# Sliding-window attention: convolutions that read the projections in PSUM, with the bias carried in closed form

## The reference

```
q = x @ Wq.T + bq ; k = x @ Wk.T + bk ; v = x @ Wv.T + bv      # x is layer-normalised first
y[t] = sum_i w[:, i] * q[t - 3 + i] + b                        # causal depthwise convolution, 4 taps,
                                                               # rows before t = 0 are zeros; also for k and v
q, k = rotary(q, k) ; q = l2norm(q) ; k = l2norm(k)
scores = q k^T / 8 , allowed where j <= i and i - j < 64
out = softmax(scores) @ v
x = x + out @ Wo.T + bo
```

## Time and profile before

| | |
|---|---|
| median of 3 runs | 2964.65 us (2958.33 to 2971.37) |
| the profiled execution | 2957.25 us, span 2955.9 us |
| the sliding attention within it, first projection to last update of x | 855 to 1337 us |
| first pairs of the two streams (A and B start 33 us apart) | 855 and 888 to 1093 and 1099 us |
| second pairs (start 5 us apart) | 1098 and 1103 to 1335 and 1337 us |

### The profile page before, as it was taken

One profiled execution on the slowest core, in us unless ns is written; L12 is line 12 of the kernel. 1 busy time (PEld: TensorE's weight loads), 2 busy tenths in 40 slices (PEclk: granted clock), 3 DMA queues, 4 the chain that ended last, 5 costly groups with the idle time before them and its releaser, 6 DMA issues. The chain is left out here.

```text
span 2955.9 us, 40949 instructions
## 1 busy us (share of the span) xinstructions
PE 2287.9 (77%) x15598; PEld 1476.6 (50%) x15598; DVE 1866.6 (63%) x3594; ACT 1356.9 (46%) x2546; POOL 695.9 (24%) x610
## 2 busy tenths in 40 slices
PE   4777839574948887885888689766778989779889
PEld 1222439454934544453586368445455554555554
DVE  6989824493438978879898899753562242652331
ACT  4545304231427877873652464344334333435342
POOL 2727340404042212216591066000010100100000
PEclk9989969786969998996897699778789999899899
DMA  4000047304832111110000000202000000000000
GB/s 175 0 0 1 1 134 234 99 1 152 241 93 87 43 33 40 40 33 5 0 1 1 0 1 1 70 1 68 13 1 1 1 2 1 8 1 1 1 1 7
DMA packets 70708, 117.80 MB, mean 40 GB/s; under 512 B 9616, under 2 KB 46224, under 8 KB 70160
## 3 DMA queue, kind: packets, MB, share of 16 engines
q1 hardware_dynamic: 64112, 104.69, 12.0%
q0 software_dynamic: 4096, 8.40, 0.9%
q10 hardware_dynamic: 2304, 2.10, 0.3%
HBM read 84.61 MB, written 16.78 MB: 34 GB/s over the span
## 5 line engine op out<-in xcount | busy, mean ns | idle before, releaser
L185 DVE SCALAR_TENSOR_TENSOR conv<-conv_in,held_l1a,conv 128x512 f32<-128x512 f32 x288 | 244.2, 871 | 29.4 <-ACT conv L166 26.4
L179 POOL TENSOR_TENSOR long<-long,product 128x512 f32<-128x512 f32 x136 | 214.1, 1593 | 198.9 <-ACT product L166 190.4
L209 POOL MEMSET wide_q<- 128x1536 f32 x8 | 11.0, 1379 | 887.1 <-DVE stream_b L182 837.3
L179 POOL TENSOR_TENSOR part<-state,c_rows 128x512 f32<-128x512 f32 x128 | 161.1, 1285 | 72.1 <-issue 53.0
L179 POOL TENSOR_TENSOR qk<-conv,held_const 128x512 f32<-128x512 f32 x64 | 92.3, 1443 | 349.4 <-DVE conv L185 349.4
L182 DVE TENSOR_SCALAR grown<-grown 128x512 f32<-128x512 f32 x92 | 39.6, 430 | 210.6 <-ACT grown L166 163.7
L148 PE MATMUL ps<-part,held_const 128*128 128x512 f32 x256 | 147.1, 659 | 13.3 <-POOL part L179 8.4
L191 DVE TENSOR_TENSOR_SCAN state<-decay,ps 128x512 f32<-128x512 f32 x128 | 146.9, 1193 | 0.0
L188 DVE TENSOR_REDUCE wide_q<-ps 128x4 f32<-128x512 f32 (+1 forms) x128 | 113.5, 950 | 49.8 <-PE ps L148 49.8
L166 ACT ACTIVATE probs<-ps 128x768 f32<-128x768 f32 x128 | 96.5, 808 | 88.2 <-PE ps L148 88.0
L148 PE MATMUL ps<-yn,nT 128*128 128x192 f32 (+2 forms) x640 | 115.6, 313 | 20.3 <-DVE yn L179 17.6
(11 more groups left out here) (503 smaller groups left out, 6135.2 us busy)
## 6 DMA issues: line engine op xcount, KB each, us to landing
ring_a<-in_experts SPq DMA_DIRECT2D x46, 512.0 KB
ring_b<-in_experts SPq DMA_DIRECT2D x46, 512.0 KB
turned<-conv SPq DMA_DIRECT2D x256, 64.0 KB
ring<-lags SPq DMA_DIRECT2D x64, 128.0 KB
held_l3f<-in_l3f SPq DMA_DIRECT2D x1, 2824.0 KB
xg<-rows_x_a SPq DMA_DIRECT2D x10, 256.0 KB
xg<-rows_x_b SPq DMA_DIRECT2D x10, 256.0 KB, 5.2
rows_y_a<-y SPq DMA_DIRECT2D x10, 256.0 KB, 5.4
```

The costliest lines, as they stand in the source:

```text
L179: return self.vector(self.real.tensor_tensor(out, a, b, op), columns(out), out, a, b)
L185: return self.vector(self.real.scalar_tensor_tensor(out, a, p, b, first, second), columns(out) + 60, out, a, b)
L209: return self.vector(self.real.memset(out, value), columns(out) // 2, out)
```

## The change

`conv_in` and the copy are gone. ScalarE's one activation reads the projection in PSUM and writes tap 3 (the unshifted one) with one bias, `whole`: the projection bias times the sum of the four taps, plus the convolution bias. VectorE adds taps 0, 1 and 2 directly from PSUM, each to the columns from 3, 2 and 1 on. Since `whole` counts the bias in all four taps, a fourth, small operation adds `gone` (minus the bias times the missing taps) to the first three columns of both sequences. `whole` and `gone` are made once per pair by seven small VectorE operations. `s.convolved` now counts four for each tile. Bank 1 comes free after the fourth (`free[0] = s.convolved, TAPS * (k + 1)`). The order of the programs changes too: on TensorE the projection of k stands behind the first mix, that of v behind the second score, and both lengths behind the second mix. ScalarE's begins and roots are moved to match. The diff, without renamed counts:

```diff
-    b = a.many(conv_in=[P, 2, SEQS, 3 + T], conv=[P, 4, TOK], turned=[P, 2, TOK], qk=[P, 2, 2, TOK],
+    b = a.many(sums=[P, 2, 3 * CT], gone=[P, 3, 3 * CT], whole=[P, 3 * CT], conv=[P, 4, TOK], turned=[P, 2, TOK], qk=[P, 2, 2, TOK],
...
+    TAPS = 4
+    tap = lambda i: w.l1_taps.rearrange("p (j i) -> p i j", i=TAPS)[:, i, :]
...
-            free[0] = s.copied, k + 1
+            free[0] = s.convolved, TAPS * (k + 1)
...
             yield from score(2 * g)
             if more:
                 yield from project(3 * g + 3)
-                yield from project(3 * g + 4)
             yield from mix(2 * g)
             if more:
+                yield from project(3 * g + 4)
+            yield from score(2 * g + 1)
+            if more:
                 yield from project(3 * g + 5)
-            yield from score(2 * g + 1)
+            yield from mix(2 * g + 1)
             if more:
                 yield from lengths_q(g + 1)
                 yield from lengths_k(g + 1)
-            yield from mix(2 * g + 1)
-            if more:
                 yield from turn_v(g + 1)
             yield from give(g)
...
-        def copy(k):
+        def begin(k):
             g, r = divmod(k, 3)
             j = r * CT + g
+            yield act.wait_ge(s.prepared, 5)
             yield act.wait_ge(s.projected, k + 1)
-            yield act.wait_ge(s.cleared, 1)
-            if k >= 2:
-                yield act.wait_ge(s.convolved, 3 * (k - 1))
-            act.activation(b.conv_in[:, k % 2, :, 3:], seqs(st.ps(1)), ACT.Identity,
-                           bias=w.l1_bqkv[:, j:j + 1]).then_inc(s.copied)
-            yield act.wait_ge(s.copied, k + 1)
             if k >= 4:
                 before = k - 4
                 if before % 3 == 2:
@@ -1302,12 +1299,12 @@
                 else:
                     yield act.wait_ge(s.cosed, 2 * (before // 3) + before % 3 + 1)
                     yield act.wait_ge(turns[before % 3], 64 * (turned_before + before // 3 + 1))
-            act.activation(seqs(b.conv[:, place(k), :]), b.conv_in[:, k % 2, :, 0:T], ACT.Identity,
-                           bias=w.l1_tap_bias[:, j:j + 1], scale=w.l1_taps[:, 4 * j:4 * j + 1]).then_inc(s.begun)
+            act.activation(b.conv[:, place(k), :], st.ps(1), ACT.Identity, bias=b.whole[:, j:j + 1],
+                           scale=w.l1_taps[:, TAPS * j + 3:TAPS * j + 4]).then_inc(s.begun)
...
             yield from exps(2 * g)
             if more:
-                yield from copy(3 * g + 3)
-                yield from copy(3 * g + 4)
+                yield from begin(3 * g + 3)
             yield from invert(2 * g)
             if more:
+                yield from begin(3 * g + 4)
                 yield from square(g + 1, 0)
             yield from exps(2 * g + 1)
             if more:
-                yield from copy(3 * g + 5)
+                yield from begin(3 * g + 5)
                 yield from square(g + 1, 1)
-                yield from roots(g + 1)
             yield from invert(2 * g + 1)
             if more:
+                yield from roots(g + 1)
                 yield from keep_v(g + 1)
...
-        ve.memset(b.conv_in[:, :, :, 0:3], 0.0).then_inc(s.cleared)
+        step = Steps(s.prepared)
+        yield step(ve.tensor_tensor(b.sums[:, 1, :], tap(0), tap(1), ALU.add))
+        yield step(ve.tensor_tensor(b.sums[:, 0, :], b.sums[:, 1, :], tap(2), ALU.add))
+        yield step(ve.tensor_tensor(b.whole[:, :], b.sums[:, 0, :], tap(3), ALU.add))
+        yield step(ve.tensor_tensor(b.whole[:, :], b.whole[:, :], w.l1_bqkv, ALU.mult))
+        ve.scalar_tensor_tensor(b.gone[:, 0:2, :], b.sums[:, 0:2, :], -1.0,
+                                w.l1_bqkv.unsqueeze(1).to_broadcast([P, 2, 3 * CT]), ALU.mult, ALU.mult
+                                ).then_inc(s.gone)
+        ve.scalar_tensor_tensor(b.gone[:, 2, :], tap(0), -1.0, w.l1_bqkv, ALU.mult, ALU.mult).then_inc(s.gone)
+        yield step(ve.tensor_tensor(b.whole[:, :], b.whole[:, :], w.l1_tap_bias, ALU.add))
...
             out = seqs(b.conv[:, place(k), :])
-            for i in range(1, 4):
-                if i == 1:
-                    yield ve.wait_ge(s.begun, k + 1)
-                else:
-                    yield ve.wait_ge(s.convolved, 3 * k + i - 1)
-                ve.scalar_tensor_tensor(out, b.conv_in[:, k % 2, :, i:i + T], w.l1_taps[:, 4 * j + i:4 * j + i + 1],
-                                        out, ALU.mult, ALU.add).then_inc(s.convolved)
+            src = seqs(st.ps(1))
+            first = b.gone[:, :, j].unsqueeze(1).to_broadcast([P, SEQS, 3])
+            yield ve.wait_ge(s.begun, k + 1)
+            yield ve.wait_ge(s.gone, 2)
+            for i in range(3):
+                if i:
+                    yield ve.wait_ge(s.convolved, TAPS * k + 1 + i)
+                late = 3 - i
+                ve.scalar_tensor_tensor(out[:, :, late:], src[:, :, 0:T - late], w.l1_taps[:, TAPS * j + i:TAPS * j + i + 1],
+                                        out[:, :, late:], ALU.mult, ALU.add).then_inc(s.convolved)
+                if i == 0:
+                    ve.tensor_tensor(out[:, :, 0:3], out[:, :, 0:3], first, ALU.add).then_inc(s.convolved)
```

More of the change, by code:

```diff
@@ L1156, in windowed_attention @@
     RING = 2
-    L = Layer(m, NORM + "cleared projected copied begun convolved squared fill_q fill_k fill_v root_log root "
+    L = Layer(m, NORM + "projected prepared gone begun convolved squared fill_q fill_k fill_v root_log root "
               "k_log k_root v_copied cosed sined rotated scaled scores exps mixed sum_log inverse normed out kept "
@@ L1208, in turn_v @@
             k = 3 * g + 2
-            yield pe.wait_ge(s.convolved, 3 * (k + 1))
+            yield pe.wait_ge(s.convolved, TAPS * (k + 1))
             yield pe.wait_ge(*free[0])
@@ L1304, in copy @@
                     yield act.wait_ge(turns[before % 3], 64 * (turned_before + before // 3 + 1))
-            act.activation(seqs(b.conv[:, place(k), :]), b.conv_in[:, k % 2, :, 0:T], ACT.Identity,
-                           bias=w.l1_tap_bias[:, j:j + 1], scale=w.l1_taps[:, 4 * j:4 * j + 1]).then_inc(s.begun)
+            act.activation(b.conv[:, place(k), :], st.ps(1), ACT.Identity, bias=b.whole[:, j:j + 1],
+                           scale=w.l1_taps[:, TAPS * j + 3:TAPS * j + 4]).then_inc(s.begun)
         def square(g, r):
             k = 3 * g + r
-            yield act.wait_ge(s.convolved, 3 * (k + 1))
+            yield act.wait_ge(s.convolved, TAPS * (k + 1))
             if g >= 1:
@@ L1355, in scalar @@
         for k in range(3):
-            yield from copy(k)
+            yield from begin(k)
             if k < 2:
@@ L1452, in pool @@
             for r in range(2):
-                yield po.wait_ge(s.convolved, 3 * (3 * g + r + 1))
+                yield po.wait_ge(s.convolved, TAPS * (3 * g + r + 1))
                 if g >= 2:
@@ L1463, in sync @@
                 k = 3 * g + r
-                yield sp.wait_ge(s.convolved, 3 * (k + 1))
+                yield sp.wait_ge(s.convolved, TAPS * (k + 1))
                 if g >= 1:
```

## The result

The changed kernel takes 3024.15 us as the median of 4 runs (3007.3 to 3038.73), against 2968.01 us for the kernel before beside it. The ratio is 1.0206, with a 95% interval of 1.0182 to 1.0231. It is slower by four times the 0.5% that such a measurement can tell, and outside the range that was predicted. The lower end of the interval is just under 2%. The profiled execution has a span of 3019.6 us, 63.7 more than before.

A forecast was written before the change was run, and what follows sets the result against it. VectorE was taken to bound the first pairs, no engine the second. First pairs -0.7, second -6.3 and starts +5 summed to -2 us: profiled 2957.3 to about 2955, median 2962.5 us, range 2932 to 2995.

The forecast's parts named there:

- 14 + 12: VectorE: 96 small sums at 150 ns each, 14 us, plus 12 us for meeting GpSimd.
- Starts: Start of each pair: lengths_q and first score wait for v's taps, +2.5 us twice, ends 0 and +8 in all.
- the loop itself: One stream's loop over bank 1, three tiles plus 6.9 us of hand-overs: grows from 12.7 to 20.3 us.
- the rivals' centres: Whole kernel: ScalarE's relief in full, 2943 us, chance 0.30; the bank 1 loop as bound, 2990 us, chance 0.20.
- if half of that is met ... I take 25.0, nearer to the floor: First pairs: half of 12.3 us of delays gives 26.4 us; 25.0 taken, floor 24.5, for 7 x -0.1 = -0.7 us.
- 4.8 to spare: First pairs: the 20.3 us loop over bank 1, alone, fits into the 25.1 us round with 4.8 us left.
- the loop becomes the bound: Rival, bank 1: first pairs 26.4 us, second 28.5, starts +8, in all +25 us, 2990; chance 0.20.
- rounds over 27 with VectorE under 80% busy: Steady rounds in the layer: named beforehand as a sign that the forecast is wrong and the bank 1 loop decides.
- streams in the first pairs lay well apart: First pairs: the reason given for taking 25.0 us a round, nearer the 24.5 us floor than 26.4.
- second pairs as one round: Second pairs: 26.4 us a round taken, low end 24.5, high end 28.5; 7 x -0.9 = -6.3 us.
- layout at +-8 us: Rest of the program, laid out anew by the planner: priced at nothing, with +-8 us.

The follow-up runs named there:

- early-release kernel: Changed kernel, but ScalarE also copies the projection to SBUF, taps read that copy and bank 1 is free after it: 1.0055 of before.
- one stream alone: Changed kernel and kernel before, each with stream B's layer waiting until stream A is through: A's rounds 20.3 and 20.6 us at clock 0.90 (changed), mean 18.9 (before, first pairs).
- half the raise: Planner's modelled costs in this layer raised by half the amounts of the full raise, only the layout changing: kernel before 1.0210, changed kernel 1.0173.
- one tap: Kernel before with the new order of TensorE's and ScalarE's programs and bank 1 held until the first of three taps: 1.0011 of before.
- Two banks: Changed kernel with projections alternating between banks 0 and 1, output projections moved to the pair's end: 1.0188 of before; with the planner's raised costs 0.9995.
- The hold alone: Kernel before, old order and copy kept, with bank 1 free only after the last tap: 3050.09 against 2930.89 us, 1.0394.
- third-tap kernel: Kernel before with the new order of TensorE's and ScalarE's programs and bank 1 held until the third tap, copies kept: 1.0274 of before.
- raised costs: Planner's modelled costs in this layer raised towards the trace's durations, only the layout changing: full raise gives changed kernel 1.0122, kernel before 1.0134.
- four layouts: Both kernels with planner's costs raised by none, half, full, one and a half: before 1, 1.0210, 1.0134, 1.0183; changed 1.0206, 1.0173, 1.0122, 1.0238.

## Why the prediction was wrong

**Right: the operations.** Taps: 742 ns on the mean, at most 750, so the contention with GpSimd went and the PSUM source costs nothing. By the rule of the Trainium skill (VectorE: DVE Perf Modes, the section on the TRN2 errata), weighed in the prediction, they would be some 65 ns dearer than from SBUF, an estimate. They are not: 744 ns at the median, against 746 for the same columns from SBUF in the early-release kernel. Small sums: 156 ns at the median, 229 on the mean because some are caught, 22.0 us, where 14 + 12 was taken. VectorE's work, by mean times count, went from 250.8 to 213.7 + 22.0, -15 us (predicted -10). ScalarE: 784 ns a begin (778), 117.45 us in 180 / 27.9 rounds, 18.2 us a round (18). Starts: +4.4 and -0.9 us (+2.5 each).

The same taps reach 1773 ns from an SBUF copy and 750 from PSUM. The Trainium skill (SBUF — State Buffer, Who interferes with whom) says that a VectorE instruction with two SBUF inputs contends with a GpSimd instruction that reads SBUF and that one with at most one such input, outside its 2-port modes, does not. The early-release kernel agrees with it.

**Right: the loop itself.** 20.3 us were added up from single operations, 20.3 and 20.6 are measured with one stream alone near the full clock. Two slips in the text change nothing: the copies of the earlier trace rows are stream B's (A's steady rounds are 25.1 us too), and the range 2932 to 2995 reaches past the rivals' centres by 11 and 5 us, not by 8.

**Wrong: what the other stream adds to the loop.** This is the step "if half of that is met ... I take 25.0, nearer to the floor". The loop was laid beside the round (20.3 in 25.1, "4.8 to spare") and its delays, though put at up to 12.3 us, were then taken at 4.7 in the first pairs. Measured are 7.4, six tenths of the 12.3. The runs with one stream alone say more: before, a lone round is 18.9 us and one with both streams 25.1, so the other stream takes 6.2 us also from a chain that the prediction did not look at. The round of 25.1 us was read as VectorE's, in which a loop of 20.3 has room; but a lone loop is fairly compared only with a lone round: 20.3 against 18.9 gives +1.4 us a round, the right sign and half of the measured 2.8. The rival "the loop becomes the bound" had the mechanism and its deciding point (4.8 us) right, but its 26.4 us for the first pairs was too low as well (27.9). The sign its text hangs on it, "rounds over 27 with VectorE under 80% busy", is what the trace shows: 27.9 and 77%. That sign is weaker than it looks, since the kernel before at half the raise comes near it with no hold (rounds of 27 us, VectorE 82% busy). The idea that streams in the first pairs lay well apart had no hold either: in the steady rounds one stream's copies of v stand 9.2 us behind the other's before, and 7.04 after.

**Wrong: second pairs as one round.** The forecast knew one round for both streams (26.4, at most 28.5). In the trace B takes 23.0 and A 31.2; their mean, 27.1, is what both took before (27.0 for A), but the later one ends the layer. That the streams come apart is not the hold's work alone: in the early-release kernel, whose layer is 481.1 us, A takes 29.9 us and B 23.6. So of the 29.0 us in A's second rounds some is order of precedence, not work. How much can't be told from these traces.

**Wrong: the layout at +-8 us.** Behind the layer, where the two kernels issue the same instructions, +15.8 us appeared. Over the profiled kernels with the bank held to the end (eight) this part averages 1631.6 us (1614.4 to 1639.9), over those without or with one tap (seven) 1631.5 (1614.1 to 1649.9). Two banks give 1630.8 and 1621.7. So these 15.8 us are not the held bank's doing; whether they are layout, or the scatter between executions of one kernel (up to 31 us), one execution can't tell. Inside the layer layouts of one kernel spread over 30 to 50 us. An edit here that makes the planner start anew needed up to 61 us of room for that alone (1.021 for the kernel before), and on the slow side.

**What is shown and what stays open.** Shown: with the planner's costs as written, the hold to the last tap is what makes the layer long. Three kernels that free the bank at the copy have layers of 480.8 to 481.1 us, five that hold it (old or new order, SBUF or PSUM source, small sums or none, output projections moved) 525.2 to 572.2. The hold alone costs 3.9% in time and the third-tap kernel 2.7%, more than any layout of the kernel before did (2.1%). And over the two groups of eight and seven kernels named above, raised costs included, the layer is 535.0 us on the mean with the bank held to the end (508.9 to 572.2) and 496.7 without (480.8 to 528.3).

Open: how much of the change's own 2.1% is the loop's length, and how much that the planner happens to find a good layout for the one and not the other. With raised costs the difference is -3 to +13 us, and on the mean of four layouts the span differs by 14 us, 0.5%, instead of 2.1%. Open too is why two banks without the raised costs win so little time. Longer rounds by the loop and layouts that leave engines idle look the same in the windows.

## What to carry over

Before a copy out of PSUM is saved, write down who needs the bank next and add up one full turn of that bank, consumer by consumer; then add what the other stream puts in its way at every step, here six tenths of what can be met, and compare with the round. Better still, compare it with a round of one stream alone. Here a turn of some 17.5 us (one tap) stayed under the 18.9 of a lone round and cost next to nothing in time, while one of 20.3 went over it and lengthened the steady rounds by 2.8 us, although 25.1 us seemed to leave it room. (The 17.5 us are an estimate; that kernel was not run with one stream alone.) And where a planner lays out the program, try the edit under several layouts before its time is believed, since here the unchanged kernel slowed by up to 2% when only modelled costs changed.

## What the runs showed of the hardware

Behind the layer the same matmuls take different time with the granted clock. The part from the layer's end to a common later sum, for before, changed, changed with full and with half raise (columns as in the earlier trace rows):

```profile
1336.00:2017.70 681.70, 516.37 (x3464) 376.48 (x3468) 579.06 (x990) 320.21 (x541) 273.28 (x212) 0.81 0.03 9
```

```profile
1383.90:2067.50 683.60, 527.85 (x3459) 382.77 (x3461) 572.97 (x939) 320.83 (x529) 270.31 (x212) 0.80 0.03 9
```

```profile
1338.00:2013.70 675.70, 510.14 (x3463) 376.37 (x3466) 570.44 (x983) 331.81 (x546) 279.00 (x212) 0.82 0.03 9
```

```profile
1372.60:2077.70 705.10, 543.82 (x3462) 397.45 (x3465) 576.28 (x982) 325.17 (x543) 275.40 (x212) 0.77 0.03 9
```

The common sum is the `x<-x,held_rows` of 128x2048 behind the layers. Some 3460 matmuls in each: 510.1 us busy at a mean clock of 0.82, 543.8 at 0.77, and the stretch is 29 us longer. The mean is one of times at the full level (2.4 GHz) and at half of it (1.2 GHz); a projection of this layer takes 592 ns at the one and 1219 at the other. Four executions of the changed kernel itself go the same way, from 3007.3 us at 0.877 to 3038.7 at 0.863. Whether the layout lowers the clock, or idle time that has another cause lowers both, was not told apart.

GpSimd gains nothing from the taps' move: its 64 products have a mean of 1455 ns, against 1443. What the taps no longer give way to, others meet: the small sum of six columns lasts up to 806 ns instead of 156.
